# Attention rows rewritten: scores as four matmuls of 32 rows, attended values made transposed, softmax sums taken in the exponential, exponentials turned by plain fp32 matmuls

## The chip, the cores and the metric

The kernel runs on one core of one Trainium2 chip. Its time is the device time of one execution in microseconds (us), as the median of repeated runs. The kernel before takes 2908.41 us (three runs, 2905.04 to 2917.83).

## The reference, cut to what matters

The whole program is a four-block network on an image of 128 rows s with 128 positions q and 64 features: row attention, a recurrence, a state-space layer run in both directions, and a mixture of eight experts. The change touches only the row attention, of which this is the computation (H = 4 heads, C = 32 channels a head, x already layer-normed):

```python
q = (x @ Wq * C ** (-0.5)).reshape(n, s, s, H, C)
k = (x @ Wk).reshape(n, s, s, H, C)
v = (x @ Wv).reshape(n, s, s, H, C)
dpa = jnp.einsum('nsqhc,nsvhc->nsqvh', k, q)
pair_bias = x @ Wb
bias = 1000000000.0 * (mask - 1.0)
dpa = dpa + bias[:, None, :, :, None]
attention = jax.nn.softmax(dpa + pair_bias[:, None], axis=3)
out = jnp.einsum('nsqvh,nsvhc->nsqhc', attention, v)
fu = jax.nn.sigmoid(x @ Wu + bu).reshape(n, s, s, H, C)
out = (out * fu).reshape(n, s, s, H * C) @ Wo + bo
out = out * mask[..., None]          # and the residual x is added
```

## The kernel before

The stages run one after another with a barrier between them. In the attention stage, `norm_stage` first makes the transposed normed input xT and the pair bias. `attention_rows`, the part that changes, then walks the 128 rows in 32 groups of GR = 4. Each engine has its own instruction list, written out by hand with semaphores; `row_steps` unrolls two groups at each end and loops over pairs of groups between. In step r an engine works on several rows at once, each at another point of the pipeline: `has(n)` says that the row n steps back exists.

TensorE in step r (all fp32): `score(r)`, one matmul of 512 columns whose stationary operand is kT of the row (128 channels of all heads by 128 positions) and whose moving operand qd holds q block-diagonally, so that each head meets only its own 32 channels; `turn(r-2)`, four transposes of the exponentials; `attend(r-3)`, four matmuls with the turned exponentials stationary and 33 moving columns (32 values and a column of ones, which gives the sum); `values_gate(r)`, one matmul of 256 columns (K = 65: values and the gate's argument); `turn_output(r-4)`; `project_output(r-5)`. Twice in a group, at j = 1 and 2, `project` makes q and k of the next group (K = 64, 512 columns).

ScalarE in step r: `exponentiate(r-1)`; at j = 2 the four copies that lay q out block-diagonally, at j = 3 the copy of k; `take_turned`; `values` (copy and tanh); `take_output`. VectorE: `add_to_x(r-6)`, `add_bias(r)`, `invert_sums(r-3)`, `apply_gate(r-3)`, `maximum(r)`, `add_output_bias(r)`, `normalise(r-3)`. GpSimd subtracts the maximum from the scores. SyncE loads two groups of xT ahead.

Of the kernel before, what the change touches and what calls it, by code (L numbers as in the profile page):

```python
# [20 lines left out]
LAG = 6  # L21
# [343 lines left out]
def row_steps(eng, step):  # L365

    def group(g, k, pair, has=lambda j: lambda lag: True):
        for j in range(GR):
            step(g * GR + j, j, g, k, has(j), pair)
    group(0, 0, 0, lambda j: lambda lag: lag <= j)  # L370
    group(1, 1, 1, lambda j: lambda lag: lag <= GR + j)
    with eng.Fori(1, NG // 2 - 1) as i:
        group(2 * i, 0, i)
        group(2 * i + 1, 1, i + 1)
    group(NG - 2, 0, NG // 2 - 1)
    group(NG - 1, 1, None)
    for d in range(LAG):
        step(S + d, d % GR, None, None, lambda lag: lag > d, None)


def attention_rows(nc, c, xT, xg, wq, wk, wvu, wo, bo_all, maskT, bias):

    with ExitStack() as ctx:
        def sb(name, shape, dt=F32):
            return ctx.enter_context(nc.sbuf_tensor(name, shape, dt))
        kT = sb("ar_kT", [128, 2, GT])
        qd = sb("ar_qd", [128, 2, GR, HEADS, 128])
        va = sb("ar_va", [128, GR, HEADS, HC + 1])
        gate = sb("ar_gate", [128, GR, 128])
        sc = sb("ar_sc", [128, GR, HEADS, 128])  # L390
        mx = sb("ar_mx", [128, GR, HEADS])
        ex = sb("ar_ex", [128, 2, HEADS, 128])
        exT = sb("ar_exT", [128, 2, HEADS * 128])
        rs = sb("ar_rs", [128, 2, HEADS])
        og = sb("ar_og", [128, 2, 128])
        og2 = sb("ar_og2", [128, 2, 128])
        ogT = sb("ar_ogT", [128, 2, 128])
        ps_s = ctx.enter_context(nc.psum_tensor("ar_pss", [128, 2, HEADS, 128], F32))
# [4 lines left out]
        ps_ot = ctx.enter_context(nc.psum_tensor("ar_psot", [128, 512], F32))  # L403
        ps_y = ctx.enter_context(nc.psum_tensor("ar_psy", [128, 512], F32))
        o_v = ps_o[:, 0:HEADS * (HC + 1)].rearrange("p (h c) -> p h c", h=HEADS)
        o_t = ps_ot[:, 0:128]
        o_y = ps_y[:, 0:D]
        sem = lambda n: c.sem("ar_" + n)

        g_proj, g_taken = sem("g_proj"), sem("g_taken")  # L410
        g_loaded = [sem("g_loaded0"), sem("g_loaded1")]

        (scored, vu_made, v_taken, g_made, added, maxed, shifted, exped, e_turned, e_taken, o_made,
         summed, gated, scaled, o_turned, o_taken, y_made, x_done, biased, ones_set) = (
            sem(n) for n in ("scored", "vu", "v", "g", "added", "maxed", "shifted", "exped", "e_turned", "e_taken",
                             "o", "summed", "gated", "scaled", "o_turned", "o_taken", "y", "x", "biased", "ones"))
        block = ctx.enter_context(nc.Block())
        SCALE = float(HC) ** -0.5

        @block.sync  # L420
        def _(sp):
            def load(g, k):
                need(sp, vu_made, GR * (g - 1))
                sp.dma_start(xg[0:D, k, :], xT[:, bass.ds(g * GT, GT)]).then_inc(g_loaded[k], 16)
# [8 lines left out]
        def _(pe):  # L433
            def project(g, k, which, pair):
                pe.wait_ge(g_loaded[k], 16 * (pair + 1))
                need(pe, g_taken, 2 * g + which)
                nc.tensor.matmul(ps_p[:, :], lhsT=(wq, wk)[which][:, :], rhs=xg[0:D, k, :],
                                 start=True, stop=True).then_inc(g_proj, 1)

            def score(r, j, g, k):  # L440
                pe.wait_ge(g_taken, 2 * (g + 1))
                need(pe, added, r - 1)
# [3 lines left out]
            def values_gate(r, j, k):  # L446
                need(pe, v_taken, r)
                need(pe, g_made, r)
                nc.tensor.matmul(ps_v[:, 0:256], lhsT=xg[0:D + 1, k, j * 128:(j + 1) * 128], rhs=wvu[:, :],
                                 start=True, stop=True).then_inc(vu_made, 1)  # L450
# [18 lines left out]
            def turn_output(r, j):  # L469
                pe.wait_ge(scaled, r + 1)  # L470
                need(pe, o_taken, r)
                nc.tensor.transpose(o_t, og2[:, j % 2, :], c.ident[:, :]).then_inc(o_turned, 1)

            def project_output(r, j):
                pe.wait_ge(o_taken, r + 1)
                need(pe, x_done, r)
                nc.tensor.matmul(o_y, lhsT=ogT[:, j % 2, :], rhs=wo[:, :], start=True, stop=True).then_inc(y_made, 1)

            def step(r, j, g, k, has, pair):

                if has(0):
                    score(r, j, g, k)
# [4 lines left out]
                if has(0):  # L487
                    values_gate(r, j, k)
                if has(4):
                    turn_output(r - 4, j)  # L490
                if has(5):
                    project_output(r - 5, (j - 5) % GR)
                if pair is not None and j in (1, 2):
                    project(g + 1, 1 - k, j - 1, pair)
            pe.wait_ge(ones_set, 2)
            project(0, 0, 0, 0)
            project(0, 0, 1, 0)
# [3 lines left out]
        def _(dve):  # L501
            nc.vector.memset(va[:, :, :, HC:HC + 1], 1.0).then_inc(ones_set, 1)
            nc.vector.memset(qd[:, :, :, :, :], 0.0).then_inc(ones_set, 1)

            def add_bias(r, j):
                dve.wait_ge(scored, r + 1)
                need(dve, exped, r - 3)
                nc.vector.tensor_tensor(sc[:, j, :, :], ps_s[:, j % 2, :, :], bias[:, :, :], ALU.add).then_inc(added, 1)  # L508

            def maximum(r, j):  # L510
                dve.wait_ge(added, r + 1)
                need(dve, shifted, r - 3)
                nc.vector.reduce_max(mx[:, j, :], sc[:, j, :, :], AX.X).then_inc(maxed, 1)  # L513

            def invert_sums(r, j):
                dve.wait_ge(o_made, r + 1)
                need(dve, scaled, r - 1)
                nc.vector.reciprocal(rs[:, j % 2, :], o_v[:, :, HC]).then_inc(summed, 1)

            def apply_gate(r, j):  # L520

                dve.wait_ge(g_made, r + 1)
                need(dve, scaled, r - 1)
                nc.vector.scalar_tensor_tensor(
                    out=og[:, j % 2, :].rearrange("p (h c) -> p h c", h=HEADS),
                    in0=gate[:, j, :].rearrange("p (h c) -> p h c", h=HEADS), scalar=1.0, in1=o_v[:, :, 0:HC],
                    op0=ALU.add, op1=ALU.mult).then_inc(gated, 1)

            def normalise(r, j):
                b = j % 2  # L530
                dve.wait_ge(gated, r + 1)
                dve.wait_ge(summed, r + 1)
                need(dve, o_turned, r - 1)
                nc.vector.tensor_tensor(og2[:, b, :].rearrange("p (h c) -> p h c", h=HEADS),
                                        og[:, b, :].rearrange("p (h c) -> p h c", h=HEADS),
                                        rs[:, b, :].rearrange("p (h a) -> p h a", a=1).to_broadcast([128, HEADS, HC]),
                                        ALU.mult).then_inc(scaled, 1)

            def add_output_bias(r):
                xr = c.x[:, bass.ds(r, 1), :].rearrange("p a d -> p (a d)")  # L540
                nc.vector.scalar_tensor_tensor(out=xr, in0=bo_all[:, :], scalar=maskT[:, bass.ds(r, 1)], in1=xr,
                                               op0=ALU.mult, op1=ALU.add).then_inc(biased, 1)

            def add_to_x(r):
# [3 lines left out]
                nc.vector.scalar_tensor_tensor(out=xr, in0=o_y, scalar=maskT[:, bass.ds(r, 1)], in1=xr,  # L548
                                               op0=ALU.mult, op1=ALU.add).then_inc(x_done, 1)

            def step(r, j, g, k, has, pair):
                if has(6):
                    add_to_x(r - 6)
                if has(0):
                    add_bias(r, j)
                if has(3):
                    invert_sums(r - 3, (j - 3) % GR)
                    apply_gate(r - 3, (j - 3) % GR)
                if has(0):
                    maximum(r, j)  # L560
                    add_output_bias(r)
# [6 lines left out]
        def _(pool):  # L568
            with pool.Fori(0, NG) as g:
                for j in range(GR):  # L570
                    pool.wait_ge(maxed, g * GR + j + 1)
                    nc.gpsimd.tensor_tensor(sc[:, j, :, :], sc[:, j, :, :],  # L572
                                            mx[:, j, :].rearrange("p (h a) -> p h a", a=1).to_broadcast([128, HEADS, 128]),
                                            ALU.subtract).then_inc(shifted, 1)

        @block.scalar
        def _(act):
            def take(g, k, which):
                act.wait_ge(g_proj, 2 * g + which + 1)
                need(act, scored, GR * (g - 1))  # L580
                if which == 0:
                    for h in range(HEADS):
                        p = slice(HC * h, HC * (h + 1))
# [1359 lines left out]
```

## Time and profile before

| | us |
|---|---|
| median of three runs | 2908.41 |
| the profiled execution's own time | 2923.91 |
| span of its profile | 2922.0 |
| mean granted TensorE clock | 0.922 of full |
| first to last `score` of the attention rows | 479.4 |

In a profile, PE is TensorE's matmuls, PEld its loads of the stationary operand, DVE VectorE, ACT ScalarE, POOL GpSimd. An fp32 matmul appears as two matmul instructions, each with a load; a transpose as one. The ends of matmuls are modelled, so the distance from one start to the next is the safer reading. The clock is 1.00 at 2.4 GHz and 0.50 at 1.2 GHz.

### The profile page before, as it was taken

How to read it: one execution, taken by the hardware profiler on the slowest of the kernel's cores; microseconds unless marked ns; L12 is line 12 of the kernel's file. 1: busy time of each engine (PE TensorE's matmuls, PEld its weight loads, DVE VectorE, ACT ScalarE, POOL GpSimd, SP SyncE). 2: the span in 40 equal slices, each digit the busy share in tenths (PEclk: the TensorE clock that was granted, in tenths of full speed). 3: DMA queues.
4: the chain of work that ended last, by engine and by line, in shares of the span. 5: the costliest groups of instructions: out<-in, count | busy, mean ns of one | idle time of the engine just before them, and what ended most of it. 6: DMA issues, size and time to landing. Idle time of an engine off the chain costs nothing. (4 is left out here: it accounts for less than half of the span.)

```text
span 2922.0 us, 39180 instructions
## 1 busy us (share of the span) xinstructions
PE 2596.1 (89%) x9464; PEld 1367.4 (47%) x9464; DVE 2244.4 (77%) x2423; ACT 1906.3 (65%) x3872; POOL 1942.9 (66%) x1102
## 2 busy tenths in 40 slices
PE   7899999958559999999999869999999999998598
PEld 7666666634324344343443324444444444447422
DVE  4266566561549999999999938899899899894599
ACT  6466566652567778788787748777777777764221
POOL 3133333230139989999999948898898898893155
PEclk6699999969679999999999979999999999996599
DMA  3000000000146667677676636666666666650022
GB/s 61 7 9 9 9 9 9 8 1 0 24 129 220 227 220 230 220 230 225 221 229 228 213 123 211 208 223 215 205 219 225 205 215 218 215 195 2 15 54 47
DMA packets 168087, 404.27 MB, mean 138 GB/s; under 512 B 64614, under 2 KB 69195, under 8 KB 168012
## 3 DMA queue, kind: packets, MB, share of 16 engines
q1 hardware_dynamic: 149580, 395.02, 42.5%
q10 hardware_dynamic: 18432, 8.39, 1.2%
q8 instruction: 29, 0.48, 0.1%
q14 instruction: 46, 0.38, 0.0%
HBM read 370.84 MB, written 24.12 MB: 135 GB/s over the span
## 5 line engine op out<-in xcount | busy, mean ns | idle before, releaser
L1496 POOL TENSOR_TENSOR sb_hc<-sb_h,sb_cc 128x1024 f32<-128x1024 f32 x256 | 602.2, 2366 | 92.3 <-PE sb_py L1256 78.6
L1496 POOL TENSOR_TENSOR sf_hc<-sf_h,sf_cc 128x1024 f32<-128x1024 f32 x256 | 602.0, 2369 | 55.3 <-PE sf_py L1256 34.0
L1256 PE MATMUL sf_py<-sf_hc,ident 128*128 128x512 f32 x1024 | 498.3, 613 | 0.0
L1256 PE MATMUL sb_py<-sb_hc,ident 128*128 128x512 f32 x1024 | 494.8, 609 | 0.5 <-DVE sb_yo L1541 0.5
L1577 DVE TENSOR_TENSOR_SCAN sf_h<-sf_dA,sf_state,sf_pu 128x1024 f32<-128x1024 f32 x192 | 446.4, 2339 | 18.9 <-PE sf_pu L1234 7.8
L1577 DVE TENSOR_TENSOR_SCAN sb_h<-sb_dA,sb_state,sb_pu 128x1024 f32<-128x1024 f32 x192 | 444.9, 2337 | 10.6 <-PE sb_pu L1234 1.3
L572 POOL TENSOR_TENSOR ar_sc<-ar_sc,ar_mx 128x512 f32<-128x512 f32 x128 | 154.9, 1210 | 363.7 <-DVE ar_mx L513 363.7
L1256 PEld LDWEIGHTS sf_py<-sf_hc,ident 128*128 128x128 f32 x1024 | 179.8, 191 | 204.7 <-issue 200.4
L1256 PEld LDWEIGHTS sb_py<-sb_hc,ident 128*128 128x128 f32 x1024 | 178.9, 190 | 202.3 <-issue 194.7
L1406 ACT ACTIVATE sf_dA<-sf_dt,ss_A 128x1024 f32<-128x1024 f32 x192 | 219.1, 1143 | 1.4 <-issue 1.2
L1406 ACT ACTIVATE sb_dA<-sb_dt,ss_A 128x1024 f32<-128x1024 f32 x192 | 219.1, 1143 | 0.9 <-issue 0.2
L1554 DVE TENSOR_TENSOR sb_pu<-sb_pu,sb_dtx 128x1024 f32<-128x1024 f32 x128 | 155.7, 1217 | 52.5 <-PE sb_pu L1243 52.5
L508 DVE TENSOR_TENSOR ar_sc<-ar_pss,at_bias 128x512 f32<-128x512 f32 x128 | 88.6, 692 | 126.7 <-PE ar_pss L443 124.6
L1834 PE MATMUL ee_ps<-ex_we,ex_xg 128*128 128x512 f32 x256 | 143.0, 647 | 40.5 <-DMA ex_xg<-ex_xT 30.1
L1554 DVE TENSOR_TENSOR sf_pu<-sf_pu,sf_dtx 128x1024 f32<-128x1024 f32 x128 | 155.7, 1216 | 23.1 <-PE sf_pu L1243 23.1
L1577 DVE TENSOR_TENSOR_SCAN sf_h<-sf_pu,sf_state,sf_dbx 128x1024 f32<-128x1024 f32 x64 | 149.5, 2336 | 14.8 <-ACT sf_pu L1411 13.6
L610 ACT ACTIVATE ar_ex<-ar_sc 128x512 f32<-128x512 f32 x128 | 80.6, 630 | 120.3 <-POOL ar_sc L572 116.4
L1389 ACT ACTIVATE sb_sT<-sb_dtxT,sb_bT 128x128 f32<-128x128 f32 x512 | 156.4, 388 | 0.9 <-issue 0.3
L1489 POOL TENSOR_TENSOR sb_dbx<-sb_dtx,sb_bb 128x1024 f32<-128x1024 f32 x64 | 151.4, 2366 | 8.3 <-DMA sb_bb<-rows_scratch 8.3
L1389 ACT ACTIVATE sf_sT<-sf_dtxT,sf_bT 128x128 f32<-128x128 f32 x512 | 156.4, 388 | 0.2
L1489 POOL TENSOR_TENSOR sf_dbx<-sf_dtx,sf_bb 128x1024 f32<-128x1024 f32 x64 | 151.5, 2367 | 6.4 <-DMA sf_bb<-rows_scratch 6.4
L1411 ACT ACTIVATE sb_pu<-sb_dt,ss_A 128x1024 f32<-128x1024 f32 x64 | 71.3, 1114 | 126.4 <-DVE sb_h L1577 122.4
(312 smaller groups left out, 5258.9 us busy)
## 6 DMA issues: line engine op xcount, KB each, us to landing
sf_cc<-rows_scratch SPq DMA_DIRECT2D x256, 512.0 KB, 4.6
sb_cc<-rows_scratch SPq DMA_DIRECT2D x256, 512.0 KB, 4.2
sf_bb<-rows_scratch SPq DMA_DIRECT2D x64, 512.0 KB, 5.5
sb_bb<-rows_scratch SPq DMA_DIRECT2D x64, 512.0 KB, 5.1
sf_n<-n_scratch SPq DMA_DIRECT2D x32, 258.0 KB, 5.4
sb_n<-n_scratch SPq DMA_DIRECT2D x32, 258.0 KB, 5.2
y_scratch<-sf_yo SPq DMA_DIRECT2D x16, 512.0 KB, 5.4
sb_yf<-y_scratch SPq DMA_DIRECT2D x16, 512.0 KB, 6.4
```

The lines of the kernel that those rows point to most:

```text
L508: nc.vector.tensor_tensor(sc[:, j, :, :], ps_s[:, j % 2, :, :], bias[:, :, :], ALU.add).then_inc(added, 1)
L572: nc.gpsimd.tensor_tensor(sc[:, j, :, :], sc[:, j, :, :], mx[:, j, :].rearrange("p (h a) -> p h a", a=1).to_broadcast([128, HEADS, 128]), ...
L610: nc.scalar.activation(ex[:, j % 2, :, :], sc[:, j, :, :], ACT.Exp).then_inc(exped, 1)
L1256: ins = nc.tensor.matmul(p_y[:, hf], lhsT=c.ident[:, :], rhs=hc[:, s % RING, hf], start=(s == 0), stop=(s == U - 1))
L1389: ins = nc.scalar.activation(sT[:, (par * NA + r) % TURN_RING, j, :], dtxT[:, j, :], ACT.Copy, scale=bT[:, par, j, s:s + 1])
L1406: nc.scalar.activation(dA[:, BY_D.index(s) % DECAY_RING, :], dt[:, par, :], ACT.Exp, scale=k["A"][:, s:s + 1]).then_inc(v_decayed, 1)
L1411: nc.scalar.activation(p_u[s % 2][:, :], dt[:, par, :], ACT.Exp, scale=k["A"][:, s:s + 1]).then_inc(g_decayed, 1)
L1489: nc.gpsimd.tensor_tensor(dbx[:, r % B_RING, :], dtx[:, par, :], bb[:, r % B_RING, :], ALU.mult).then_inc(g_injected, 1)
L1496: nc.gpsimd.tensor_tensor(hc[:, s % RING, :], h[:, s % RING, :], cc[:, s % C_RING, :], ALU.mult).then_inc(read, 1)
L1554: nc.vector.tensor_tensor(p_u[s % 2][:, :], p_u[s % 2][:, :], dtx[:, par, :], ALU.mult).then_inc(v_injected, 1)
L1577: nc.vector.tensor_tensor_scan(out=flow(h[:, s % RING, :]), data0=flow(decays), data1=flow(inputs), initial=state[:, s:s + 1], op0=ALU.mul ...
L1834: nc.tensor.matmul(ps[:, j, :, :], lhsT=xg[:, k, j * Q:(j + 1) * Q], rhs=we[:, :, :], start=True, stop=True).then_inc(made, 1)
```

## The change

Scores: q is copied as it comes (scaled by minus the scale, one ScalarE copy in place of four) and each head has its own matmul on its 32 channels, written to a bank of its own, one buffer in place of two. VectorE subtracts the bias from the negated scores and takes the minimum. ScalarE makes the exponential with scale -1 and that minimum as its bias, one instruction a head, each with a sum output `tot`; GpSimd's subtraction goes away. The exponentials are turned by plain fp32 matmuls against the identity. `attend` has the values stationary (128 rows by the head's 32 columns) and the turned exponentials moving, which gives the output transposed; four more matmuls spread the inverted sums in the same layout. The gate is projected a group at a time, like q and k, and `turn_output` with its copy goes away. The output bias is added by GpSimd in two instructions a row. The pipeline is 5 steps deep, not 6.

```diff
-LAG = 6
+LAG = 5
-        qd = sb("ar_qd", [128, 2, GR, HEADS, 128])
-        ps_s = ctx.enter_context(nc.psum_tensor("ar_pss", [128, 2, HEADS, 128], F32))
+        qT, kT, gate = sb("ar_qT", [128, 2, GT]), sb("ar_kT", [128, 2, GT]), sb("ar_gate", [128, 2, GT])
+        ps_s = ctx.enter_context(nc.psum_tensor("ar_pss", [128, HEADS, 512], F32))
+        p_s = ps_s[:, :, 0:128]
+        p_y = ps_s[:, 0, 128:128 + D]
+        o_T, r_T = ps_o[:, 0:128], ps_o[:, 128:256]
+        band = [slice(HC * h, HC * (h + 1)) for h in range(HEADS)]
+        tile = lambda j: slice(j * 128, (j + 1) * 128)
...
+            def project_u(g, k):
+                pe.wait_ge(k_taken, g + 1)
+                nc.tensor.matmul(ps_p[:, :], lhsT=wvu[:, 128:256], rhs=xg[0:D + 1, k, :], start=True,
+                                 stop=True).then_inc(u_made, 1)
...
             def score(r, j, g, k):
-                nc.tensor.matmul(ps_s[:, j % 2, :, :], lhsT=kT[:, k, j * 128:(j + 1) * 128],
-                                 rhs=qd[:, k, j, :, :], start=True, stop=True).then_inc(scored, 1)
+                for h in range(HEADS):
+                    ins = nc.tensor.matmul(ps_s[:, h, 0:128], lhsT=kT[band[h], k, tile(j)], rhs=qT[band[h], k, tile(j)],
+                                           start=True, stop=True)
+                ins.then_inc(scored, 1)
...
+            def values(r, j, k):
+                nc.tensor.matmul(ps_v[:, 0:128], lhsT=xg[0:D, k, tile(j)], rhs=wvu[0:D, 0:128],
+                                 start=True, stop=True).then_inc(v_made, 1)
...
             def turn(r, j):
-                    ins = nc.tensor.transpose(ps_t[:, h * 128:(h + 1) * 128], ex[:, j % 2, h, :], c.ident[:, :])
+                    ins = nc.tensor.matmul(ps_t[:, tile(h)], lhsT=ex[:, j % 2, h, :], rhs=c.ident[:, :],
+                                           start=True, stop=True)
...
             def attend(r, j):
                 pe.wait_ge(e_taken, r + 1)
                 pe.wait_ge(v_taken, r + 1)
-                need(pe, gated, r)
-                need(pe, summed, r)
+                pe.wait_ge(inverted, r + 1)
+                need(pe, scaled, r)
                 for h in range(HEADS):
-                    ins = nc.tensor.matmul(o_v[:, h, :], lhsT=exT[:, j % 2, h * 128:(h + 1) * 128],
-                                           rhs=va[:, j, h, :], start=True, stop=True)
+                    nc.tensor.matmul(ps_o[band[h], 0:128], lhsT=va[:, j, band[h]], rhs=exT[:, j % 2, tile(h)],
+                                     start=True, stop=True)
+                for h in range(HEADS):
+                    ins = nc.tensor.matmul(ps_o[band[h], 128:256], lhsT=rs[:, j % 2, h:h + 1].to_broadcast([128, HC]),
+                                           rhs=c.ident[:, :], start=True, stop=True)
                 ins.then_inc(o_made, 1)
...
             def step(r, j, g, k, has, pair):
                 if has(0):
+                    need(pe, added, r)
+                if has(5):
+                    project_output(r - 5, (j - 5) % GR)
+                if has(0):
+                    need(pe, x_done, r - 5)
                     score(r, j, g, k)
...
-                if has(4):
-                    turn_output(r - 4, j)
-                if pair is not None and j in (1, 2):
-                    project(g + 1, 1 - k, j - 1, pair)
+                if pair is not None:
+                    if j == 1:
+                        project_q(g + 1, 1 - k, pair)
+                    if j == 2:
+                        project_k(g + 1, 1 - k)
+                    if j == 3:
+                        project_u(g + 1, 1 - k)
...
-            nc.vector.memset(qd[:, :, :, :, :], 0.0).then_inc(ones_set, 1)
+                nc.vector.tensor_tensor(sc[:, j, :, :], p_s, bias[:, :, :], ALU.subtract).then_inc(added, 1)
+                nc.vector.tensor_reduce(out=mn[:, j, :], in_=sc[:, j, :, :], axis=AX.X, op=ALU.min).then_inc(least, 1)
             def invert_sums(r, j):
+                dve.wait_ge(exped, r + 1)
+                nc.vector.reciprocal(rs[:, j % 2, :], tot[:, j % 2, :]).then_inc(inverted, 1)
...
             def exponentiate(r, j):
-                nc.scalar.activation(ex[:, j % 2, :, :], sc[:, j, :, :], ACT.Exp).then_inc(exped, 1)
+                for h in range(HEADS):
+                    ins = nc.scalar.activation(ex[:, j % 2, h, :], sc[:, j, h, :], ACT.Exp, bias=mn[:, j, h:h + 1],
+                                               scale=-1.0, accum_out=tot[:, j % 2, h:h + 1])
+                ins.then_inc(exped, 1)
```

VectorE's order becomes `add_bias(r)`, `add_to_x(r-5)`, `invert_sums(r-2)`, `apply_gate(r-3)`, `minimum(r)`, `normalise(r-3)`; ScalarE's `exponentiate(r-1)`, one of the copies of q (j = 2), k (j = 3) and the gate (j = 0), `take_turned(r-2)`, `take_values(r)`. GpSimd scales and adds the output bias for four rows at a time and waits only on itself. SyncE's loads wait for `values` where they waited for `values_gate`.

## Rows read from the trace of the kernel before

**Rows 1.** The page: the span, and the granted TensorE clock by slices.
```profile
span 2922.0 us, 39180 instructions
...
PEclk6699999969679999999999979999999999996599
```

**Rows 2.** Stretches: start:end, length, busy of each engine, granted clock, DMA share, GB/s.
```profile
112.30:591.67 479.37, 468.48 (x2492) 326.06 (x2492) 283.58 (x872) 302.95 (x782) 152.44 (x126) 0.95 0.04 8
400.33:414.98 14.65, 14.30 (x83) 10.07 (x82) 9.04 (x29) 9.63 (x26) 4.86 (x4) 1.00 0.04 9
302.81:308.27 5.46, 5.46 (x20) 4.17 (x20) 1.99 (x6) 1.98 (x6) 0.35 (x2) 0.53 0.00 0
2.00:95.00 93.00, 77.70 (x380) 76.80 (x380) 33.10 (x64) 59.75 (x98) 27.28 (x23) 0.61 0.28 48
```

**Rows 3.** Waits from 400 to 500 us: who waited, for whom, us in total, times.
```profile
POOL ar_sc L572 <- DVE ar_mx L513: 68.5, 28, 3.4
PEld ar_psp L437 <- ACT ar_qd L584: 3.4, 7, 0.5
```

**Rows 4.** Timeline of TensorE over two rows: start, length, instruction.
```profile
403.29 1.08 PE L443 MATMUL ar_pss<-ar_qd,ar_kT 128*128 128x512 f32 x2
404.21 0.60 PE L456 MATMUL ar_pst<-ident,ar_ex 128*128 128x128 f32 x4
404.64 0.98 PE L465 MATMUL ar_pso<-ar_va,ar_exT 128*128 128x33 f32 x8
405.46 0.68 PE L449 MATMUL ar_psv<-at_wvu,at_xg 65*128 65x256 f32 x2
405.97 0.28 PE L472 MATMUL ar_psot<-ident,ar_og 128*128 128x128 f32 x1
406.08 0.33 PE L477 MATMUL ar_psy<-at_wo,ar_ogT 128*128 128x64 f32 x2
406.35 1.12 PE L437 MATMUL ar_psp<-at_xg,at_wq 64*128 64x512 f32 x2
407.40 1.12 PE L443 MATMUL ar_pss<-ar_qd,ar_kT 128*128 128x512 f32 x2
...
414.98 1.08 PE L443 MATMUL ar_pss<-ar_qd,ar_kT 128*128 128x512 f32 x2
...
417.94 1.08 PE L443 MATMUL ar_pss<-ar_qd,ar_kT 128*128 128x512 f32 x2
```

**Rows 5.** Timeline of TensorE in the state-space stage, full clock.
```profile
1525.98 1.02 PE L1265 MATMUL sf_py<-sf_xc,ss_dg 128*128 128x512 f32 x2
1526.84 1.88 PE L1256 MATMUL sf_py<-sf_hc,ident 128*128 128x512 f32 x4
1528.55 1.02 PE L1265 MATMUL sf_py<-sf_xc,ss_dg 128*128 128x512 f32 x2
1529.51 0.60 PE L1243 MATMUL sf_pu<-sf_bcs,ss_sel 48*128 48x512 bf16 x2
1530.04 1.98 PE L1256 MATMUL sf_py<-sf_hc,ident 128*128 128x512 f32 x4
```

**Rows 6.** ScalarE's groups of instructions, 400 to 500 us: busy us, mean ns of one.
```profile
L600 ACT COPY ar_exT<-ar_pst 128x512 f32<-128x512 f32 x27 | 15.6, 577 | 2.3 <-PE ar_pst L456 2.1
L593 ACT COPY ar_va<-ar_psv 128x128 f32<-128x128 f32 x28 | 7.5, 268 | 5.2 <-PE ar_psv L449 5.2
```

**Rows 7.** Timeline of ScalarE, two small activates in a row.
```profile
400.25 0.27 ACT L593 COPY ar_va<-ar_psv 128x128 f32<-128x128 f32 x1 [0.74 <-PE ar_psv L449]
400.41 0.28 ACT L595 ACTIVATE ar_gate<-ar_psv 128x128 f32<-128x128 f32 x1
```

**Rows 8.** Timeline of the start of the attention rows.
```profile
101.35 3.47 DVE L503 MEMSET ar_qd<- 128x4096 f32 x1 [0.80 <-issue]
...
107.05 2.39 ACT L584 ACTIVATE ar_qd<-ar_psp 32x512 f32<-32x512 f32 x4 [9.71 <-PE ar_psp L437]
...
109.58 2.04 PE L437 MATMUL ar_psp<-at_xg,at_wk 64*128 64x512 f32 x2 [2.63 <-ACT ar_qd L584]
```

More of the change, by code:

```diff
@@ L433, in _, with project_q @@
         def _(pe):
-            def project(g, k, which, pair):
+            def project_q(g, k, pair):
                 pe.wait_ge(g_loaded[k], 16 * (pair + 1))
-                need(pe, g_taken, 2 * g + which)
-                nc.tensor.matmul(ps_p[:, :], lhsT=(wq, wk)[which][:, :], rhs=xg[0:D, k, :],
-                                 start=True, stop=True).then_inc(g_proj, 1)
-            def score(r, j, g, k):
-                pe.wait_ge(g_taken, 2 * (g + 1))
-                need(pe, added, r - 1)
-                nc.tensor.matmul(ps_s[:, j % 2, :, :], lhsT=kT[:, k, j * 128:(j + 1) * 128],
-                                 rhs=qd[:, k, j, :, :], start=True, stop=True).then_inc(scored, 1)
@@ new lines, in project_output @@
+            def project_output(r, j):
+                pe.wait_ge(scaled, r + 1)
+                need(pe, x_done, r)
+                nc.tensor.matmul(p_y, lhsT=og2[:, j % 2, :], rhs=wo[:, :], start=True, stop=True).then_inc(y_made, 1)
+            def score(r, j, g, k):
+                pe.wait_ge(k_taken, g + 1)
+                for h in range(HEADS):
+                    ins = nc.tensor.matmul(ps_s[:, h, 0:128], lhsT=kT[band[h], k, tile(j)], rhs=qT[band[h], k, tile(j)],
+                                           start=True, stop=True)
+                ins.then_inc(scored, 1)
@@ L529, in normalise, with apply_gate @@
+                need(dve, o_made, r - 1)
+                nc.vector.reciprocal(rs[:, j % 2, :], tot[:, j % 2, :]).then_inc(inverted, 1)
+            def apply_gate(r, j, g, k):
+                dve.wait_ge(u_taken, g + 1)
+                dve.wait_ge(o_made, r + 1)
+                nc.vector.scalar_tensor_tensor(out=og[:, j % 2, :], in0=gate[:, k, tile(j)], scalar=1.0, in1=o_T,
+                                               op0=ALU.add, op1=ALU.mult).then_inc(gated, 1)
             def normalise(r, j):
-                b = j % 2
+                need(dve, y_made, r - 1)
@@ L531, in normalise @@
                 dve.wait_ge(gated, r + 1)
[L532 to L542, printed above, removed]
+                nc.vector.tensor_tensor(og2[:, j % 2, :], og[:, j % 2, :], r_T, ALU.mult).then_inc(scaled, 1)
             def add_to_x(r):
@@ new lines, in add_output_bias, with group @@
+            def add_output_bias(r, j):
+                pool.wait_ge(masked, r + 1)
+                xr = c.x[:, bass.ds(r, 1), :].rearrange("p a d -> p (a d)")
+                nc.gpsimd.tensor_tensor(xr, xr, bm[:, j, :], ALU.add).then_inc(biased, 1)
+            def group(g):
+                for j in range(GR):
+                    scale_bias(g * GR + j, j)
+                for j in range(GR):
+                    add_output_bias(g * GR + j, j)
+            group(0)
+            with pool.Fori(1, NG) as g:
+                group(g)
@@ L576, in _, with take_q @@
         @block.scalar
         def _(act):
-            def take(g, k, which):
-                act.wait_ge(g_proj, 2 * g + which + 1)
+            def take_q(g, k):
+                act.wait_ge(q_made, g + 1)
                 need(act, scored, GR * (g - 1))
-                if which == 0:
-                    for h in range(HEADS):
-                        p = slice(HC * h, HC * (h + 1))
-                        ins = nc.scalar.activation(qd[p, k, :, h, :], ps_p[p, :].rearrange("p (j v) -> p j v", j=GR),
-                                                   ACT.Copy, scale=SCALE)
-                else:
-                    ins = nc.scalar.copy(kT[:, k, :], ps_p[:, :])
-                ins.then_inc(g_taken, 1)
@@ L590, in values, with take_k, take_u @@
-            def values(r, j):
-                act.wait_ge(vu_made, r + 1)
+                nc.scalar.activation(qT[:, k, :], ps_p[:, :], ACT.Copy, scale=-SCALE).then_inc(q_taken, 1)
+            def take_k(g, k):
+                act.wait_ge(k_made, g + 1)
+                need(act, scored, GR * (g - 1))
+                nc.scalar.copy(kT[:, k, :], ps_p[:, :]).then_inc(k_taken, 1)
+            def take_u(g, k):
+                act.wait_ge(u_made, g + 1)
+                need(act, scaled, GR * (g - 1))
+                nc.scalar.activation(gate[:, k, :], ps_p[:, :], ACT.Tanh, scale=0.5).then_inc(u_taken, 1)
@@ L614, in step @@
                     exponentiate(r - 1, (j - 1) % GR)
-                if pair is not None and j in (2, 3):
-                    take(g + 1, 1 - k, j - 2)
+                if j == 0 and has(0) and not (isinstance(g, int) and g == 0):
+                    take_u(g, k)
+                if pair is not None and j == 2:
+                    take_q(g + 1, 1 - k)
+                if pair is not None and j == 3:
+                    take_k(g + 1, 1 - k)
                 if has(2):
@@ L619, in step @@
                 if has(0):
-                    values(r, j)
-                if has(4):
-                    take_output(r - 4, j)
-            act.wait_ge(ones_set, 2)
-            take(0, 0, 0)
-            take(0, 0, 1)
+                    take_values(r, j)
+            take_q(0, 0)
+            take_k(0, 0)
+            take_u(0, 0)
             row_steps(act, step)
```

108 lines of the change are left out of this document (38 added, 70 removed).

## The prediction

> **What bounds the kernel now.** Three kinds of view were read. First the busy time by stretches. The attention rows take 479.4 us from the first score to the last, 127 rows apart, so 3.775 us a row. TensorE is busy for 468.5 of them, VectorE for 284, ScalarE for 303, GpSimd for 152 [rows 2]. In a stretch of four rows (one group) at full clock the lengths are 14.65 us, so 3.66 a row, with TensorE busy for 14.30. Only this stage changes. What stands before and after it keeps its work and moves in time.
>
> Second the waits. GpSimd waits 68 us in 100 us for VectorE, which is idleness of an engine with nothing to do. The one wait that stops TensorE itself is that of the k projection for the block-diagonal copies of q, 3.4 us in seven groups or 0.5 a group [rows 3]. So the rows go at TensorE's pace.
>
> Third the timeline of TensorE, which gives the price of each piece as the distance between starts [rows 4]: score 0.92, turn 0.43, attend 0.82, values and gate 0.51, output's turn 0.11, output's projection 0.17 (from 406.08 to a score at the same tiling, as between 414.98 and 417.94, where a whole row takes 2.96).
>
> These starts follow one rule of thumb. The turn has four instructions of 128 columns in 0.43 us, so one costs 0.107. Attend moves only 33 columns in each of its eight instructions and still takes 0.82, so 0.103 each: there the load of 128 stationary columns sets the pace at the same 0.107. An fp32 matmul has two instructions. A matmul of 512 columns costs 0.86 (from 1525.98 to 1526.84) [rows 5]. By this rule a row is score 0.86, turn 0.43, attend 0.86, values 0.43, output's turn 0.11, output 0.21, which sums to 2.90; measured 2.96, so 0.06 is left over and is carried along.
>
> The row that also makes q is 4.11 long (403.29 to 407.40) [rows 4]: 1.15 more for a matmul worth 0.86. It has K = 64, in the midst of matmuls with K = 65 or 128. The 0.29 left over lies at its two borders. The state-space stage shows it too: before a 48-row matmul the 0.86 becomes 0.96 (1528.55 to 1529.51), and the 48-row bf16 matmul takes 0.53 (1529.51 to 1530.04) [rows 5] where two instructions of 512 columns at half the fp32 price are worth 0.43. So I take 0.15 for each change of tile shape.
>
> The Trainium skill says so in words ("TensorEngine Tiling (Array Packing)", Key Properties): changing the tiling mode, not just the tile, drains TensorE. It gives no figure; the trace agrees, with the 0.15.
>
> **The change, TensorE first.** By the rule above, with p = 0.107 for one instruction of 128 columns:
>
> Turn: 8 p = 0.86 where it was 0.43.
>
> Values: 2 p = 0.21. Output: 2 p = 0.21, as before, loads setting it. Output's turn: gone.
>
> Projections: three in a group at 0.86, so 0.645 a row, where two stood.
>
> Shape changes: a row now goes from output (128 by 128) to score (32 rows), turn (128), attend (32 columns), values (64 rows), and back. That is five, 0.75 a row. The q and k projections share the shape of values and the gate's shares that of the output, so projections add none. Before there was 0.29 twice a group.
>
> Score: four matmuls of 128 columns on 32 rows each, so eight instructions. One after another they cost 8 p = 0.86, nearly what they cost before. They use different rows of the array and different banks, so they could run beside each other; no row of before shows two matmuls that do. The other bound is that all four lie fully over each other: 2 p = 0.21. Between the ends: the two instructions of one head need the same rows of the array and must follow one another, and if the stream keeps its order only the last of one head and the first of the next can overlap. That gives 5 p = 0.535. The loads are still 128 columns wide, and if these cannot overlap the step stays at 0.86. I take the middle of these two, 0.70.
>
> Attend: eight matmuls of 128 columns on 32 columns of the array, so sixteen instructions: 16 p = 1.71 one after another, 4 p = 0.43 fully over each other, and by the same ordering 9 p = 0.96. The loads are only 32 columns wide and can't set the pace, so I take 0.96.
>
> Sum: 0.70 + 0.86 + 0.96 + 0.21 + 0.21 + 0.06 + 0.75 + 0.645 = 4.395 us a row, against 3.66. That is 0.735 a row over 127 rows, 93 us. The whole stage runs 3.775/3.66 = 1.03 times its full-clock pace, for the stretches at half clock, so 96 us.
>
> **The other engines are cover, not cost.** ScalarE was busy 9.63 us a group, 2.4 a row. Now a row has a copy of the turned exponentials, 0.58, of values, 0.27 [rows 6], and three copies of 512 columns in a group, 3 x 0.58 / 4 = 0.43. The four exponentials of 128 columns with a sum output have no row. From below they are spaced like the two small activates, 0.16 apart [rows 7]: 0.65. From above, each takes its whole 0.28 and as much again to read out its sum: 2.3. So ScalarE needs 1.9 to 3.6 a row, under 4.4 at either end. I take 2.7, in between, as nothing decides; it costs nothing.
>
> VectorE was busy 2.26 a row and loses the bias addition. GpSimd was at 1.21 for a 128x512 subtraction; two additions of an eighth of that cost at most 2.4 a row by that row and wait for nobody. The copy of q is one instruction in place of four, so the 0.5 us wait a group goes; that is in the sum, since 3.66 held it.
>
> New waits. The score waits for `add_bias` of the row before, as there is one score buffer: 0.7 us of VectorE's work, while TensorE has turn, attend and values, over 2 us, between two scores. Behind it stands TensorE's whole list. Attend waits for `normalise` of the row before: gate, minimum and product, some 1.3 us after the last attend, and TensorE's work from attend to attend without attend itself is over 3 us. It waits also for `inverted`, made a step earlier. The new projection of the gate waits for k's copy, a step earlier too. The loads of SyncE hang on `values`, one a row as before. All of these are covered as long as TensorE needs more than about 3 us a row.
>
> Start: VectorE's 3.47 us memset, on which the first projection waited until 104.88, is gone (-3.3); q's copies take 0.6, not 2.39 (-1.8); the gate's projection stands ahead of the first score, 2.04 at half clock [rows 8] (+2.0). With one step less in the pipeline at the end I take -6 in all.
>
> Total: +96 - 6 = +90 us. On the profiled execution's own 2923.9 that is 3014. The median of the runs is 15.5 below it, so 2998 for the median.
>
> The forecast's own range: shape changes at 0.10 and the score at 0.535 give 3.98 a row, +36 us, 2944; changes at 0.20 and the score at 0.86 give 4.81, +149, 3057.
>
> **Rivals.** (1) *The tiles lie fully over each other.* Score 0.21 and attend 0.43: 3.375 a row, 0.285 under before, so -37 - 6 = -43 us, 2865, faster. For it: distinct rows, columns and banks. Against it: each head's two instructions stand together in the stream. It decides once overlap saves more than 1.6 us of the serial 2.57 a row. The Trainium skill is its advocate ("TensorE: Matmul & The Clock Gate", Part 3): matmuls on different tiles start about 4 ns apart, four row tiles measured 3.07 times faster. No row here shows such a pair.
>
> (2) *The same, with ScalarE as the new bound* at its upper price, 3.6 a row: -8 - 6 = -14 us, 2894, no change.
>
> (3) *The tiles don't overlap at all*, or small instructions can't be issued faster than the 0.107 seen: 0.86 + 1.71, so 5.305 a row, +1.645 over 127 rows with the 1.03, +215 - 6, 3117.
>
> (4) *TensorE's clock.* It is granted at 0.95 in this stage, with a row at half clock taking 5.46, not 2.96. Before the stage it stood at 0.61, while the engine was busy 78 of 93 us, with its loads at 77 us [rows 2]; by slices it stays near full only from the attention rows on [rows 1]. It stands at 0.53 inside the stage too, with the engine busy throughout [rows 2]. With waits and drains in each row it may fall more. A row would take about 8 us; half the stage so would add 230 us, over 3200. It can go the other way too: 0.95 means 48 of 479 us at half clock, and without them the stage would be some 24 us shorter, which the range holds.
>
> **Chances.** The forecast (partial overlap) 0.47, (1) 0.22, (2) 0.06, (3) 0.15, (4) 0.10. A measurement of this kernel tells about 0.5% (14.5 us) from no change. Faster is (1) with a little of the forecast's lower end: 0.23. Same is (2) with as little: 0.07. Slower 0.70. The range must leave out no more than 0.2, so it holds all but (4) and the far ends: 2860 to 3125. The likeliest case's own is 2944 to 3057.
>
> **What would show it.** In the profile after: the distance between scores, 4.4 us on average; the score's eight instructions 0.54 to 0.86 from first to the turn's first, less 0.15; attend's sixteen near 0.96 (0.43 for rival 1, 1.71 for rival 3); a gap of 0.10 to 0.20 with the load not pulled ahead at each of five borders a row; turn 0.86. ScalarE idle before its exponentials, waiting for the minimum. The granted clock near 0.95. It is wrong if starts of the tiles lie a few ns apart, if TensorE waits for ScalarE or VectorE in every row, or if the clock reads 0.5 for long.

## The result, and the profile after

The kernel before took 2913.12 us (median of 4 runs), the changed one 2886.11 (4 runs, 2883.33 to 2887.02): a ratio of 0.990, 95% interval 0.9865 to 0.9935. It is faster by 27 us, where 90 us slower was forecast. The profiled execution took 2886.68 with a span of 2884.6.

First the stage in stretches (start:end, length, busy time of PE, PEld, DVE, ACT and POOL, granted clock): all rows, and one group of four rows at full clock, which answer to the first two of [rows 2].

```profile
111.00:565.00 454.00, 453.91 (x4715) 315.85 (x4716) 258.87 (x754) 356.02 (x1363) 56.77 (x216) 0.97 0.04 9
401.37:415.45 14.08, 14.08 (x151) 9.82 (x150) 8.18 (x25) 11.25 (x44) 0.00 (x0) 1.00 0.04 9
```

A group takes 14.08 us where it took 14.65, so 3.52 a row against 3.66. TensorE is busy in all of it, as before; ScalarE rose from 9.63 to 11.25 and is still under it. From the first score (110.0) to the last (562.2) there are 452.2 us, 3.561 a row against 3.775. Part of that is the group, 0.14 a row or 18 us over 127 rows. The other 9 us fit the granted clock, 0.97 over the rows where it was 0.95: after the change its only low stretch is at the start of the rows, while before it fell again inside them, as in the row of 5.46 us in [rows 2]. The next lines show it (the same columns, changed kernel).

```profile
110.00:130.00 20.00, 19.91 (x111) 12.47 (x110) 6.79 (x14) 11.24 (x43) 20.00 (x76) 0.50 0.03 7
150.00:560.00 410.00, 410.00 (x4366) 285.99 (x4366) 238.53 (x700) 327.57 (x1252) 17.77 (x68) 1.00 0.04 9
```

The first score comes 2.3 us earlier (112.3 to 110.0) and what follows the last one, up to the next stage's first sum, is 2.5 us shorter (14.4 to 11.9), so the two profiles differ by 32.0 us at the end of the stage. The other 5.4 of 37.4 came in stages that were not changed.

Then TensorE's timeline over a row that also makes q, which answers to [rows 4] (start, length, instruction), and the two starts around a row that makes no projection.

```profile
401.37 0.50 PE L455 MATMUL ar_pss<-ar_qT,ar_kT 32*128 32x128 f32 x8
401.80 1.16 PE L468 MATMUL ar_pst<-ident,ar_ex 128*128 128x128 f32 x8
402.89 0.43 PE L478 MATMUL ar_pso<-ar_exT,ar_va 128*32 128x128 f32 x8
403.13 0.40 PE L481 MATMUL ar_pso<-ident,ar_rs 128*32 128x128 f32 x8
403.47 0.48 PE L461 MATMUL ar_psv<-at_wvu,at_xg 64*128 64x128 f32 x2
403.79 1.02 PE L436 MATMUL ar_psp<-at_xg,at_wq 64*128 64x512 f32 x2
404.74 0.43 PE L450 MATMUL ar_pss<-at_wo,ar_og 128*128 128x64 f32 x2
405.11 0.50 PE L455 MATMUL ar_pss<-ar_qT,ar_kT 32*128 32x128 f32 x8
...
412.58 0.50 PE L455 MATMUL ar_pss<-ar_qT,ar_kT 32*128 32x128 f32 x8
...
415.45 0.50 PE L455 MATMUL ar_pss<-ar_qT,ar_kT 32*128 32x128 f32 x8
```

Read the starts. Eight matmuls of the attended values take 0.24 us, up to the start of the eight for the sums: two instructions of 0.107 and little more, so four heads lie beside each other. The score's eight take 0.43 with the border behind them. The turn takes 1.09, its 0.86 and a border. A row with a projection is 3.74 long, one without it 2.87.

The same timeline cut at single instants counts how many of the score's instructions had started. First what had started by 401.39, then by 401.48, then the matmuls by 401.57 and by 401.62, and last all the loads:

```profile
401.37 0.39 PE L455 MATMUL ar_pss<-ar_qT,ar_kT 32*128 32x128 f32 x3
401.37 0.20 PEld L455 LDWEIGHTS ar_pss<-ar_qT,ar_kT 32*128 32x128 f32 x4
...
401.37 0.39 PE L455 MATMUL ar_pss<-ar_qT,ar_kT 32*128 32x128 f32 x4
401.37 0.29 PEld L455 LDWEIGHTS ar_pss<-ar_qT,ar_kT 32*128 32x128 f32 x5
...
401.37 0.39 PE L455 MATMUL ar_pss<-ar_qT,ar_kT 32*128 32x128 f32 x4
...
401.37 0.50 PE L455 MATMUL ar_pss<-ar_qT,ar_kT 32*128 32x128 f32 x8
...
401.37 0.31 PEld L455 LDWEIGHTS ar_pss<-ar_qT,ar_kT 32*128 32x128 f32 x8
```

By 401.39 four loads and three matmuls have started, and the fourth matmul by 401.40: four of each within 0.03 us. The fifth load follows by 401.48, 0.1 us after the first, and the last before 401.51. No fifth matmul starts before 401.57; then the second four start together, 0.2 us after the first four. The trace does not name the head of an instruction, so that each group of four has one of every head is inferred, from run 2: with all heads on one band of rows only one matmul starts in the first 0.1 us. So it is not head after head but, as far as this shows, first halves, then second halves.

ScalarE, over one row's exponentials (timeline):

```profile
401.64 0.40 ACT L615 ACTIVATE ar_ex<-ar_sc,ar_mn 128x128 f32<-128x128 f32 x1 [0.27 <-DVE ar_mn L521]
401.95 0.19 ACT L615 ACTIVATION_READ_ACCUMULATOR ar_ex<-ar_sc,ar_mn 128x1 f32 x1
402.05 0.39 ACT L615 ACTIVATE ar_ex<-ar_sc,ar_mn 128x128 f32<-128x128 f32 x1
402.34 0.19 ACT L615 ACTIVATION_READ_ACCUMULATOR ar_ex<-ar_sc,ar_mn 128x1 f32 x1
402.43 0.39 ACT L615 ACTIVATE ar_ex<-ar_sc,ar_mn 128x128 f32<-128x128 f32 x1
```

Each exponential with its sum is 0.39 from the next, so four cost 1.56 us where one of 512 columns took 0.63.

### The profile page after: what moved, and what is told of

It reads as the page before. It is cut to its first block and busy times, and to the rows that moved or that the text cites. A ratio compares the mean times of both kernels' runs of the same rounds, so it can differ in the third digit from the quotient of the medians.

```text
span 2884.6 us, 43927 instructions
## 1 busy us (share of the span) xinstructions
PE 2576.6 (89%) x11704; PEld 1350.8 (47%) x11704; DVE 2213.0 (77%) x2293; ACT 1956.1 (68%) x4448; POOL 1854.5 (64%) x1230
## 5 line engine op out<-in xcount | busy, mean ns | idle before, releaser
L615 ACT ACTIVATE ar_ex<-ar_sc,ar_mn 128x128 f32<-128x128 f32 x512 | 199.1, 390 | 43.7 <-DVE ar_mn L521 43.6
```

The lines of the kernel that those rows point to most:

```text
L615: ins = nc.scalar.activation(ex[:, j % 2, h, :], sc[:, j, h, :], ACT.Exp, bias=mn[:, j, h:h + 1], scale=-1.0, accum_out=tot[:, j % 2, h:h ...
```

## The experiments

The runs carry the numbers of their labels; there is no sixth. Each was timed beside the kernel before, and its ratio is to that (medians of before 2916.5, 2913.8 and 2913.1 in the three sessions). Pitch is the distance from first to last score over 127; it is 3.775 before and 3.561 after. The theory was by now that the tiles lie fully over each other and that TensorE still sets every row's pace (A); the rivals were that the overlap isn't what it seems, that ScalarE or the chain through VectorE is as near, or that the clock moves.

**Run 2: the score on one band of rows.**

```diff
-  lhsT=kT[band[h], k, tile(j)], rhs=qT[band[h], k, tile(j)]
+  lhsT=kT[band[0], k, tile(j)], rhs=qT[band[0], k, tile(j)]
```

> All four score matmuls of a row read the first 32 channels (head 0), so all stand on the same 32 rows of the array; sizes, banks, waits and shape changes stay, the scores of heads 1 to 3 are those of head 0. Theory A (the tiles of after really run beside each other, 2 x 0.107 us for four heads, and TensorE sets the pace): the score goes from 0.21 to 0.86 us without its border, +0.64 a row, +82 us, near 2968. Rival: they don't need distinct rows to overlap, or the 0.43 measured is mostly the border: no change to +20 us.

Measured: 2972.63 us, ratio 1.0203 (1.0179 to 1.0227), 87 us over after; pitch 4.190.

```profile
399.98 0.96 PEld L455 LDWEIGHTS ar_pss<-ar_qT,ar_kT 32*128 32x128 f32 x8
399.99 1.15 PE L455 MATMUL ar_pss<-ar_qT,ar_kT 32*128 32x128 f32 x8
401.07 1.16 PE L468 MATMUL ar_pst<-ident,ar_ex 128*128 128x128 f32 x8
```

The same eight matmuls take 1.08 us to the turn where they took 0.43, and their loads 0.96 where they took 0.31. The 0.65 is the six of eight that no longer overlap, and all of it reaches the end. So distinct rows are what makes them overlap, and it is worth 87 us.

**Run 3: attend on one band of columns.** The attended values of this kernel are not the reference's: all heads write the first 32 partitions.

```diff
-  nc.tensor.matmul(ps_o[band[h], 0:128], lhsT=va[:, j, band[h]], ...
+  nc.tensor.matmul(ps_o[band[0], tile(h)], lhsT=va[:, j, band[h]], ...
-  ins = nc.tensor.matmul(ps_o[band[h], 128:256], lhsT=rs[...], ...
+  ins = nc.tensor.matmul(ps_o[band[0], tile(h)], lhsT=rs[...], ...
```

> All eight matmuls of attend write the first 32 output partitions (column tile 0), each head 128 columns further on in the bank, so they can't lie beside each other; a memset of the bank stands ahead once. The attended values are then not the reference's. Theory A: attend goes from 2 x 0.21 to 16 x 0.107 = 1.71 us, +1.28 a row, +163 us, near 3049. Rival: the chain of ScalarE and VectorE had slack to give or column tiles overlap in part only, and it is under +100 us.

Measured: 3046.19 us, ratio 1.0455 (1.0432 to 1.0479), 160 us over after; pitch 4.775.

```profile
400.04 1.06 PE L479 MATMUL ar_pso<-ar_exT,ar_va 128*32 128x128 f32 x8
400.94 1.04 PE L482 MATMUL ar_pso<-ident,ar_rs 128*32 128x128 f32 x8
401.90 0.48 PE L462 MATMUL ar_psv<-at_wvu,at_xg 64*128 64x128 f32 x2
```

0.90 and 0.96 where it was 0.24 and 0.34. Runs 2 and 3 together price the overlap at 247 us.

**Run 4: one change of shape less.**

```diff
-  lhsT=xg[0:D, k, tile(j)], rhs=wvu[0:D, 0:128]
+  lhsT=xg[0:D + 1, k, tile(j)], rhs=wvu[:, 0:128]
-  lhsT=wq[:, :], rhs=xg[0:D, k, :]          # and wk
+  lhsT=wq[:, :], rhs=xg[0:D + 1, k, :]      # row D of wq, wk is zero
```

> Values and the q and k projections with K = 65 (a row of zeros added to the weights), so they share the 128-row shape of the output projection that follows: four changes of tile shape a row in place of five, the same columns and instructions. Theory A: a border costs about 0.2 us on TensorE's path, so -0.2 a row, -25 us, near 2861. Rival: the gap ahead of the output projection is its wait for VectorE's normalise, not the shape, and nothing moves.

Measured: 2857.15 us, ratio 0.9811 (0.979 to 0.9831), 29 us under after; pitch 3.329, so 0.23 less a row. Two starts of its score, around a row with the gate's projection:

```profile
400.68 0.50 PE L457 MATMUL ar_pss<-ar_qT,ar_kT 32*128 32x128 f32 x8
...
404.23 0.50 PE L457 MATMUL ar_pss<-ar_qT,ar_kT 32*128 32x128 f32 x8
```

3.55 where after has 3.74: a border is on the path and costs 0.19, rather than the 0.15 of the forecast. The other 0.04 of the pitch fits the clock, 0.98 against 0.97.

**Run 1: the turn by transposes again.**

```diff
-  ins = nc.tensor.matmul(ps_t[:, tile(h)], lhsT=ex[:, j % 2, h, :], rhs=c.ident[:, :], start=True, stop=True)
+  ins = nc.tensor.transpose(ps_t[:, tile(h)], ex[:, j % 2, h, :], c.ident[:, :])
```

> The changed kernel with its exponentials turned by transposes again, nothing else. Theory A: TensorE sets the pace of every row (3.52 us a row after), and each plain fp32 matmul of 128 columns costs two instructions of 0.107 us where a transpose costs one; a row gets 0.43 us shorter, 3.09, and the kernel 127 x 0.43 = 55 us faster than after, near 2831. Rival B: ScalarE, busy 2.81 us a row after with its four exponentials and their sum reads, or the round through VectorE, takes over before that; the pitch stays above 3.2 and the gain is under 35 us. Rival C: with transposes the granted clock falls inside the rows as it did before the change (0.95 over the rows) and eats 10 us or more of it.

Measured: 3114.85 us, ratio 1.0667 (1.0635 to 1.0698), 229 us slower than after instead of 55 faster; pitch 5.335. First its timeline, then a stretch of 530 us.

```profile
406.35 0.81 PE L455 MATMUL ar_pss<-ar_qT,ar_kT 32*128 32x128 f32 x8
407.09 1.11 PE L468 MATMUL ar_pst<-ident,ar_ex 128*128 128x128 f32 x4
408.13 0.66 PE L477 MATMUL ar_pso<-ar_exT,ar_va 128*32 128x128 f32 x8
...
410.49 0.81 PE L455 MATMUL ar_pss<-ar_qT,ar_kT 32*128 32x128 f32 x8
...
110.00:640.00 530.00, 529.91 (x3263) 312.86 (x3263) 200.34 (x582) 281.75 (x1063) 57.88 (x219) 0.50 0.03 6
```

TensorE is busy in all of 530 us and has no wait to speak of, but its clock is granted at 0.50 throughout, 1.2 GHz. A row without a projection takes 4.14 us, not the 2.44 that theory A gives it at full clock (2.87 less 0.43): 1.7 times as long, not twice. Rival C, in a size that it did not name: not dips but the whole stage. So the turn's plain matmuls cost 0.43 us a row, and in this kernel the other 2.44 ran at full clock only where some of them were kept. One thing this run leaves open: the kernel before, the changed one and runs 1 and 9 to 11 all enter the rows at 0.50. The changed kernel and runs 9 to 11 are at 1.00 by 140 us and stay there to their last row, and the kernel before, with its four transposes, is there at 130; run 1 never rises. So what is shown is that its clock did not come up; whether it would have come down from full clock is not.

**Run 9: two heads of four transposed.**

```diff
+  if h < 2:
+      nc.tensor.transpose(ps_t[:, tile(h)], ex[:, j % 2, h, :], c.ident[:, :])
+  else:
       ins = nc.tensor.matmul(ps_t[:, tile(h)], lhsT=ex[:, j % 2, h, :], rhs=c.ident[:, :], ...
```

> The changed kernel with two heads turned by transposes and two by plain matmuls, nothing else. If the clock holds: -0.21 a row, -27 us, near 2859. If it falls as in the first run: 2 x 3.3 us a row, above 3100. In between would show a clock that changes back and forth in the rows.

Measured: 2848.45 us, ratio 0.9774 (0.9749 to 0.9799), 38 us under after; pitch 3.283, clock 0.97 over the rows, as after. Two starts of its score, around a row without a projection:

```profile
401.88 0.50 PE L455 MATMUL ar_pss<-ar_qT,ar_kT 32*128 32x128 f32 x8
...
404.48 0.50 PE L455 MATMUL ar_pss<-ar_qT,ar_kT 32*128 32x128 f32 x8
```

That row is 2.60 us long where it was 2.87: two transposes save 0.27, somewhat more than the 0.21 expected, and what the other 0.06 is was not found. It is not the mere presence of transposes that holds the clock down.

**Run 8: transposes, and more of something else.** The edits of runs 1 and 2 together.

> The first run's transposes together with the second run's score on one band of rows (scores of heads 1 to 3 are those of head 0): more columns one after another on TensorE, nothing saved. If it is what stays of TensorE's streaming that decides the clock, the clock of the rows rises from the first run's 0.50 to near 1, a row takes 3.09 + 0.64 = 3.73 us, and the kernel is near 2913, 200 us faster than the first run though it does more. If transposes by themselves bring the clock down, the row gets 1.28 longer at half clock and the kernel is near 3275.

Measured: 3277.28 us, ratio 1.1244 (1.1211 to 1.1277); pitch 6.605, clock 0.50. The second branch came out to 2 us. Its pitch is 1.27 us over that of run 1, six instructions at twice 0.107, and that much more streaming on 32 rows did not lift the clock. The kernel before has four transposes too, beside a score of 512 columns on all 128 rows, and stood at 0.95. Which of its differences from run 1 decides was not taken apart and stays open.

**Run 12: the kernel before with the plain turn.** The edit is that of this change alone, on the kernel before.

> The kernel before with its exponentials turned by plain fp32 matmuls, nothing else. Theory A: 0.43 us a row more on TensorE's path, +55 us, and up to 24 us of it given back if the stretches at half clock inside the rows vanish: 2945 to 2970. Rival: the transposes held the clock down for more of the time than the trace of before shows, and it comes out at 2930 or less.

Measured: 2947.1 us, ratio 1.0112 (1.0079 to 1.0145); pitch 3.996. Timeline, then the stretch of its rows:

```profile
400.64 1.08 PE L443 MATMUL ar_pss<-ar_qd,ar_kT 128*128 128x512 f32 x2
401.55 1.05 PE L456 MATMUL ar_pst<-ident,ar_ex 128*128 128x128 f32 x8
...
404.05 1.08 PE L443 MATMUL ar_pss<-ar_qd,ar_kT 128*128 128x512 f32 x2
...
113.00:620.00 507.00, 505.45 (x2993) 378.39 (x2992) 284.47 (x874) 303.97 (x784) 152.08 (x127) 0.99 0.04 8
```

A row without a projection is 3.41 where it was 2.96 [rows 4], +0.45 as the term says. The pitch rose by 0.22 only. Two things give the rest back: the clock went from 0.95 to 0.99, and the wait for q's copies, 0.5 us a group or 0.13 a row in [rows 3], is no longer among TensorE's waits. So the expected time was met with one term of it, the wait, left out. On the old kernel the plain turn costs 34 us; on the new one it saves 229.

**Run 5: three changes of shape.** On top of run 4:

```diff
   # TensorE, step r
-  output(r-5); score(r); turn(r-2); attend(r-3); values(r); project
+  turn(r-2); values(r); project; output(r-5); attend(r-3); score(r)
   # VectorE, step r
+  add_to_x(r-5); invert_sums(r-2); apply_gate(r-3); normalise(r-3); add_bias(r); minimum(r)
```

> On top of the fourth run, TensorE's order in a step becomes turn, values, projections, output (all 128 by 128), then attend, then score: three changes of shape a row in place of four. VectorE's order follows (adds to x, sums, gate, product, bias, minimum). Theory A: one border less, 0.2 us a row, -25 us against the fourth run, near 2832. Rival B: the score at the end of a step leaves VectorE and ScalarE less time before the next turn (ScalarE busy 2.8 of a 3.2 us row), so waits for exponentials or their copy take it back: 2845 or more.

Measured: 3151.37 us, ratio 1.0816 (1.0789 to 1.0843); pitch 5.645. Its waits from 400 to 500 us (who, for whom, us in total, times, longest):

```profile
DVE x_tok L545 <- PE ar_pss L452: 52.8, 19, 4.8
ACT ar_ex L615 <- DVE ar_mn L523: 51.6, 18, 5.2
PEld ar_psp L442 <- ACT ar_qT L588: 10.7, 4, 2.7
PEld ar_psp L446 <- ACT ar_kT L593: 7.9, 5, 1.7
...
110.00:820.00 710.00, 570.28 (x4631) 412.31 (x4634) 283.14 (x738) 328.21 (x1339) 57.37 (x218) 0.73 0.03 6
```

Rival B, and far worse than it said. The projection of k waits for q's copy, which stands behind the exponentials in ScalarE's list, which wait for the minimum of a score that now comes last in the step. TensorE is busy for only 570 of 710 us, and its clock with gaps in it is at 0.73: the wait is paid twice.

**Run 13: the same with the copies first in ScalarE's list.**

> The fifth run with ScalarE's copies of q, k and the gate ahead of the exponentials in its list. Theory A: what stopped TensorE there was the projection waiting for a copy that stood behind the exponentials, which wait for the score made last in the step before; with the copies first those waits of 3.5 us a group and more go, and the time falls under 2950. Rival B: the chain score, bias, minimum, exponentials, turn has no step of slack left in that order, TensorE still idles each row, and the clock stays low with it: above 3050.

Measured: 2922.35 us, ratio 1.0025 (1.0007 to 1.0043); pitch 3.969, clock 0.91.

```profile
PEld ar_pst L470 <- ACT ar_ex L615: 51.4, 52, 1.5
PE ar_pst L470 <- ACT ar_exT L608: 44.0, 55, 1.4
...
110.00:590.00 480.00, 426.19 (x4466) 315.87 (x4465) 269.83 (x713) 320.17 (x1298) 56.20 (x214) 0.91 0.04 8
```

229 us came back, so theory A holds for what stopped run 5; the waits for the copies of q and k are gone. What is left is the waiting that rival B named, though not the time above 3050 that it gave: TensorE's matmuls are idle for 54 of 480 us. The two waits shown, of the turn's loads for the exponentials and of its matmuls for the copy, lie in the same gaps and don't add up. The order has no slack left, and loses to run 4, which has one border more.

**Run 7: run 5 with two heads transposed.**

> On top of the fifth run, two of the four heads' exponentials are turned by transposes, two by plain fp32 matmuls. If the clock stays at 2.4 GHz and TensorE still sets the pace: -0.21 a row, -27 us, near 2805. If ScalarE's 2.8 us a row and its waits set the pace by now: within 10 us of the fifth run. If the granted clock falls in the rows as in the first run: above 3000.

Measured: 3173.37 us, ratio 1.089 (1.0859 to 1.0922); pitch 5.883. Less work and 22 us slower than run 5. It comes nearest to the last branch: TensorE is busy for 585 of 740 us (570 of 710 in run 5) and its clock is down from 0.73 to 0.64. But run 5 was above 3000 already, so the branches no longer part cleanly. In an order that already left gaps, shorter streaming bought nothing, and the clock stood lower; whether the waits or the clock moved first was not taken apart.

**Runs 10 and 11: the best of both.** K = 65 as in run 4, with two and with three heads of four transposed.

> The fourth run (K = 65, four changes of shape a row) and the ninth (two heads turned by transposes) together. Theory A, TensorE sets the pace at full clock: -29 and -38 us add up, near 2819, 3.06 us a row. Rival B: ScalarE, busy 2.76 us a row in the ninth run, takes over: 2835 or more, with TensorE waiting for exponentials. Rival C: the granted clock falls in the rows: above 3000.

> As the tenth run, with three heads of four turned by transposes. If the clock holds: another -0.11 a row, -14 us, near 2805, if ScalarE lets it. If it falls as with four transposes in the first run: above 3000. In between: it falls in parts of the rows.

Measured: 2823.97 us, ratio 0.9695 (0.9665 to 0.9725), and 2811.04, ratio 0.9647 (0.9616 to 0.9678); pitches 3.054 and 2.993. First run 10, then run 11:

```profile
110.00:495.00 385.00, 384.91 (x4408) 275.00 (x4408) 253.51 (x745) 337.61 (x1347) 56.24 (x214) 0.99 0.05 11
```

```profile
110.00:480.00 370.00, 370.00 (x4198) 258.95 (x4199) 247.76 (x728) 328.08 (x1321) 55.99 (x213) 0.97 0.05 11
```

The savings of runs 4 and 9 nearly add up (29 + 38, measured 62), and run 11 is the fastest version found, 75 us under after and 102 under before. In both TensorE is busy throughout and never waits for ScalarE, though that engine is busy 89% of run 11. The third transpose brings 13 us and not the half clock that stood beside the fourth in run 1 (there with one border more).

## Why the prediction was wrong

**The frame held.** TensorE sets the pace before and after. The waits that were called covered are covered: TensorE waits for no other engine in the rows after, and neither the single score buffer, the `normalise` of the row before nor the gate's projection shows. The part of the range above the forecast has a slip, on which nothing hangs: 4.81 us a row with the start's -6 is +144, not +149. ScalarE was put at 2.7 us a row between 1.9 and 3.6, and is busy 2.81. The four exponentials cost 1.56 us, within 0.65 to 2.3. Start and end were put at -6 and gave -4.8.

**The step that failed** is the choice between the ends for the score and for attend: "the two instructions of one head need the same rows of the array and must follow one another, and if the stream keeps its order only the last of one head and the first of the next can overlap". From this came 0.70 for the score and 0.96 for attend. The instants above show otherwise: four instructions start together, then the other four, which is what the prediction had named as a sign of being wrong. The score is worth 0.21 and attend 0.43 without their borders, the lower end of both, and runs 2 and 3 show that this overlap is what the time hangs on: taken away, it costs 87 and 160 us, the serial ends (82 and 163) within 5 us. With 0.21 and 0.43 the forecast's own sum is 3.375 a row, which was rival 1. The stated range, 2860 to 3125, holds the 2886 measured only because it was drawn wide enough to take in that rival; the forecast's own 2944 to 3057 does not. The loads, 128 columns wide in the score, overlap too. The rival was given 0.22 because no row of before shows a pair of tiles; the right reading of that was that the rows are silent, not that they speak for the middle. The page of the Trainium skill named there ("TensorE: Matmul & The Clock Gate", Part 3) describes the overlap, and the trace agrees that tiles lie over each other, for fp32 too: four starts within 0.03 us.

**The borders were under-sized.** 0.15 was taken for each. The row without a projection is 2.87 us, while its columns cost 0.21 + 0.86 + 0.43 + 0.21 + 0.21 = 1.92. That leaves 0.95, five at 0.19 on average, which is what run 4 measured for one. Against 0.06 + 0.75 in the sum it is 0.14 a row more, 18 us, and so most of the 21 us between the 2886 measured and rival 1's 2865.

**The turn** was right as a price, 0.43 a row (1.09 with its border; 0.45 measured in run 12). But its sign for the whole was not seen. It was costed as work that TensorE could do without. Run 1 shows that without it the clock of these rows stands at 0.50 and the kernel is 229 us slower. Rival 4 named the clock as a danger of the change; it proved one of undoing it. The clock's other direction was named too: 24 us at most, about 9 came.

**The projections** were right: 0.87 us for each row that has one (3.74 against 2.87), against 0.86. The half microsecond of waiting for q's copies is gone as said.

## What to carry to other kernels

Where small tiles may run beside each other and the trace has no such pair, give the two ends equal weight and work the sum at both; a middle made up from an order that no row shows is no safer. Put matmuls of one shape next to each other: on this kernel each change of shape costs about 0.2 us, and one row of zeros in the weights removed one for 29 us. Before taking work off TensorE, ask what the clock will be without it: dearer instructions in the right number can be the cheaper kernel, and the number is worth a run each, since two and three transposes of four were gains (three only tried with one border less) and four a loss of 229 us.

## What the runs showed of the hardware

With TensorE busy for all of 530 us, the granted clock stood at 0.50 in run 1, with four transposes a row. It was 0.97 to 0.99 over the rows in runs 9 to 11 with two or three and in the changed kernel with none, all of them entering at 0.50 and at 1.00 from 140 us on. Adding serial matmuls on 32 rows to run 1 (run 8) left it at 0.50. The kernel before held 0.95 with four. Busy time in the profile does not tell which level will be granted.

fp32 matmuls on four bands of rows overlap: four matmul instructions of the score start within 0.03 us, loads of 128 columns as well; the other four loads follow 0.1 us later and the other four matmuls 0.2 us later. On one band of rows the eight take 0.65 us more.

A change of tile shape costs 0.19 us at full clock in the changed kernel (run 4).

Reading a sum out of ScalarE adds an instruction of 0.19 us to each exponential and sets them 0.39 apart.
